# Second homes in dead attention buffers for the expert weights of one tile set, in an attention and mixture-of-experts kernel

## The chip, the cores and the metric

The kernel runs on one core of one Trainium2 chip. The metric is the device time of one execution in microseconds (us). Five engines run their own instruction streams and meet at semaphores: TensorE (PE; its weight loads are listed as PEld), VectorE (DVE), ScalarE (ACT), GpSimd (POOL) and SyncE (SP, which here only issues transfers). A name with q behind it (SPq, ACTq) is the engine's sequencer, where its transfers are issued. Sixteen DMA engines move the data of all queues.

## What is computed

The reference, cut to what matters (8 batches of 256 tokens with 256 features, 16 heads, 77 context keys, 16 experts with one expert per token):

```python
x = x + attention(layernorm(x), ctx, ctx, mask, Wq, bq, Wk, bk, Wv, bv, Wo, bo)
h = layernorm(x).reshape(2048, 256)
logits = h @ w_router.T                       # 16 experts
top = top_k(logits, 1)
scores = sigmoid(logits) * one_hot(top)
gate, up = split(scores.T[:, :, None] * h @ gate_up_proj)    # per expert: 256 -> 2 x 512
expert = (up * silu(gate)) @ down_proj                        # per expert: 512 -> 256
shared = silu(h @ w_gate.T) * (h @ w_up.T) @ w_down.T
x = x + (shared + expert.sum(axis=0)).reshape(8, 256, 256)
```

Everything is float32. With the reference's inputs the 16 experts get 109, 249, 79, 164, 51, 177, 57, 78, 162, 185, 87, 183, 101, 171, 104 and 91 tokens.

## The kernel before, in words

**Stages.** The first 205 us are the attention over eight batches, with the shared feed-forward of the first five batches (the "early" ones, NE = 5) woven in. Then come the shared products of the last three batches (R = 3) on PE (L778 gate and up, L790 down), beside which DVE works out the routing: where each token goes in tiles of 32 rows (TS) that belong to one expert each. Last come 20 expert steps (NSTEP).

**An expert step.** A step takes four tiles (NG) at a time, one in each quarter of PE's columns. The steps alternate between two sets of weight buffers: even steps use set A (a = 0), odd ones set B (a = 1). Step i is use u = i // 2 of its set. A set holds for each of its four tile lanes one expert's gate-and-up weights (128 x 2048 numbers, 1 MB, `w_egu`) and down weights (128 x 1024, 0.5 MB, `w_ed`). Set A lies in the buffers `own`, set B in the `arena` that attention used before. Set A's guess of the experts it will need is loaded in the attention (L307, L309 with a = 0), set B's once attention is over.

**SP's order.** SP issues, in program order, (1) the usual experts of set B, once the last attention product is out (L306 to L309); (2) after the routing is known, for use 0 of both sets the weights of those lanes whose expert differs from the guess (L337 gate and up, L342 down; each transfer carries a condition `new`, and where it is false nothing is moved, but the semaphore is raised); (3) for step i from 2 on: `gate_up_again(i)` waits until the gate-and-up products of step i - 2 have read the same buffers (`egu_psum`), `down_again(i)` until its down products have (`ed_psum`). Step i's gate and up are issued before step i - 1's down. Tiles lie in order of experts and a lane takes ten tiles in a row, so a lane's expert changes seldom. Worked out from the token counts above, the lanes with a new expert are, at uses 0 to 9: set A 2, 2, 1, 1, 2, 1, 0, 0, 0, 1; set B 1, 0, 0, 0, 0, 2, 1, 0, 0, 3.

**PE's order in the expert part.** For each step: gate and up (L862, 32 products), the previous step's down (L880, 32 products), the transposes of the next step's gathered rows (L851), and the transposes of its own hidden values (L869), for which ACT's gate and DVE's product of the same step must be done. The first products are gate-and-up 0, then L851 for step 1, L869 for step 0, gate-and-up 1, down 0, L851 for step 2, L869 for step 1, gate-and-up 2, down 1, L851 for step 3, L869 for step 2, gate-and-up 3, and so on.

**POOL's order in the expert part.** POOL issues three kinds of indirect transfers, each behind a small marker instruction (L493): `gather_rows` (L504) brings the normalised rows of a step into `xs`, `gather_base` (L512) the sums to which the result is added (`attT` is where they land), `scatter_out` (L519) writes the result. The order is rows 0, 1, 2, a wait for all eight stores of `base`, base 0, base 1, rows 3, scatter 0, base 2, rows 4, scatter 1, and so on.

**The base.** `base` is a DRAM copy of the sum of residual, attention and shared output. SP stores it for the five early batches (L301), ACT for the last three (L1021, 256 KB each, 128 x 2 pieces of 1 KB), each when DVE has added the shared output (`shared_added`). All eight raise `base_stored`.

**ACT's and DVE's orders.** ACT in the expert part: scale the rows of a step (L1031, waits for the gathered rows), gate of the step before (L1039), read out the transposed rows (L1035), read out the transposed hidden values (L1043). DVE: hidden values of step i (L1356), then the result rows of step i - 1 (L1363), which wait for the gathered base.

## Time and profile before

| what | value |
|---|---|
| time, median of 3 runs | 392.1 us (390.1 to 392.56) |
| profiled execution, its own time | 395.31 us |
| its span, first to last instruction | 393.3 us |
| mean granted TensorE clock | 0.980 of full |
| expert part on PE (first L862 to last L880) | 248.0 to 384.2 us |

A timeline row gives the start, the duration, engine, line, operation, what is written from what, how many instructions are merged, and in brackets how long the engine had been idle before and what ended that idle time. A row with "DMA own<-w_experts" in its brackets is one where PE stood and the transfer of expert weights came last. A windows row gives for a stretch of time the busy time of each engine, the granted TensorE clock as a share of full (1.00 is 2.4 GHz, 0.50 is 1.2 GHz), the busy share of the DMA engines and the bytes they moved per second.

### The profile page before, as it was taken

How to read it: one execution, taken by the hardware profiler on the slowest of the kernel's cores; microseconds unless marked ns; L12 is line 12 of the kernel's file. 1: busy time of each engine (PE TensorE's matmuls, PEld its weight loads, DVE VectorE, ACT ScalarE, POOL GpSimd, SP SyncE). 2: the span in 40 equal slices, each digit the busy share in tenths (PEclk: the TensorE clock that was granted, in tenths of full speed). 3: DMA queues.
4: the chain of work that ended last, by engine and by line, in shares of the span. 5: the costliest groups of instructions: out<-in, count | busy, mean ns of one | idle time of the engine just before them, and what ended most of it. 6: DMA issues, size and time to landing. Idle time of an engine off the chain costs nothing.

```text
span 393.3 us, 9350 instructions
## 1 busy us (share of the span) xinstructions
PE 352.2 (90%) x3068; PEld 225.3 (57%) x3068; DVE 191.6 (49%) x567; ACT 172.9 (44%) x472; POOL 159.5 (41%) x271
## 2 busy tenths in 40 slices
PE   2778788999999999998999999979998999999780
PEld 1556466777777777776776888424443434444330
DVE  2479899967967949767742852112121212111110
ACT  1258979665665565756641311312333232332310
POOL 5354656433522623422221021333656464656411
PEclk9989999999999999999999999989999999999987
DMA  8330102020069300000014999384558696314940
GB/s 239 145 85 3 44 0 72 0 72 2 27 231 408 125 0 27 27 26 3 27 55 168 397 273 363 114 343 147 184 163 287 223 350 209 106 41 159 380 197 20
DMA packets 23326, 56.47 MB, mean 144 GB/s; under 512 B 7275, under 2 KB 14461, under 8 KB 19968
## 3 DMA queue, kind: packets, MB, share of 16 engines
q1 hardware_dynamic: 16704, 48.59, 34.6%
q0 software_dynamic: 2880, 6.31, 5.0%
q10 hardware_dynamic: 3712, 1.22, 1.3%
q8 instruction: 13, 0.21, 0.2%
q14 instruction: 17, 0.14, 0.1%
HBM read 149.94 MB, written 6.82 MB: 399 GB/s over the span
## 4 chain that ended last, share of the span: by engine, by line
PE 30%; issue 27%; POOL 16%; DVE 13%; ACT 5%; DMA 5%; POOLq 1%; DVEq 0%; ACTq 0%
PE ps L651 8%; POOL xs L504 5%; POOL attT L512 5%; PE ps L657 5%; PE ps L578 4%; PE ps L593 3%; DMA rows<-score 3%; POOL pool_carrier L493 3%; POOL out L519 2%; PE ps L632 2%; DVE arena L1127 2%; PE ps L603 2%; ACT arena L935 2%; DVE den L1136 2%; DMA mask_in<-mask 2%
## 5 line engine op out<-in xcount | busy, mean ns | idle before, releaser
L451 POOL TENSOR_TENSOR arena<-arena,rden 128x308 f32<-128x308 f32 x64 | 44.7, 699 | 95.0 <-DVE rden L1140 94.3
L935 ACT ACTIVATE arena<-arena,negtop 128x77 f32<-128x77 f32 x256 | 70.6, 350 | 19.2 <-DVE negtop L1132 19.2
L1356 DVE TENSOR_TENSOR act_g<-act_g,ps 128x512 f32<-128x512 f32 x20 | 13.8, 688 | 90.9 <-PE ps L862 90.9
L493 POOL TENSOR_TENSOR pool_carrier<-neghalf 1x1 f32<-1x1 f32 x60 | 11.0, 183 | 81.2 <-DVE qT L1363 48.3
L603 PE MATMUL ps<-ident,arena 128*77 128x128 f32 x256 | 40.4, 284 | 2.1 <-ACT arena L943 2.1
L862 PE MATMUL ps<-own,qT 128*32 128x512 f32 x320 | 37.9, 615 | 4.4 <-DMA own<-w_experts 3.5
L862 PE MATMUL ps<-arena,qT 128*32 128x512 f32 x320 | 38.1, 617 | 3.8 <-DMA arena<-w_experts 3.6
L651 PE MATMUL ps<-xn2T,w_gu 128*128 (+1 forms) x160 | 39.5, 390 | 0.6 <-ACT xn2T L948 0.6
L603 PEld LDWEIGHTS ps<-ident,arena 128*77 128x77 f32 x256 | 30.0, 150 | 10.6 <-issue 6.7
L651 PEld LDWEIGHTS ps<-xn2T,w_gu 128*128 128x128 f32 x160 | 28.8, 189 | 10.0 <-issue 5.9
L1035 ACT ACTIVATE qT<-ps 128x256 f32<-128x256 f32 x20 | 7.7, 383 | 59.5 <-PE ps L851 59.5
L1127 DVE TENSOR_TENSOR arena<-ps,arena 128x308 f32<-128x308 f32 x64 | 30.0, 469 | 5.9 <-PE ps L593 5.6
L1136 DVE TENSOR_REDUCE den<-arena 128x4 f32<-128x308 f32 x64 | 29.7, 465 | 4.8 <-ACT arena L935 4.7
L593 PE MATMUL ps<-arena,qT 64*128 64x308 f32 x128 | 25.2, 471 | 6.3 <-DVE arena L1127 4.7
L1132 DVE TENSOR_REDUCE negtop<-arena 128x4 f32<-128x308 f32 x64 | 30.3, 474 | 0.1
L862 PEld LDWEIGHTS ps<-own,qT 128*32 128x32 f32 x320 | 10.9, 112 | 24.7 <-issue 20.8
L519 POOL DMA_INDIRECT out<-qT,token x20 | 20.4, 1020 | 11.3 <-issue 10.7
L862 PEld LDWEIGHTS ps<-arena,qT 128*32 128x32 f32 x320 | 9.6, 113 | 25.5 <-issue 19.5
L1039 ACT ACTIVATE act_g<-ps 128x512 f32<-128x512 f32 x20 | 11.9, 596 | 24.6 <-PE ps L862 24.5
L943 ACT ACTIVATE arena<-ps 77x512 f32<-77x512 f32 x32 | 18.7, 584 | 9.2 <-PE ps L603 9.2
L504 POOL DMA_INDIRECT xs<-rows,token x20 | 20.7, 1035 | 3.9 <-issue 1.7
L778 PE MATMUL ps<-xn2T,w_gu 128*128 128x256 f32 x96 | 22.2, 382 | 0.0
(149 smaller groups left out, 579.2 us busy)
## 6 DMA issues: line engine op xcount, KB each, us to landing
own<-w_experts SPq DMA_DIRECT2D x44, 1024.0 KB
arena<-w_experts SPq DMA_DIRECT2D x44, 1024.0 KB
own<-w_experts SPq DMA_DIRECT2D x44, 512.0 KB
arena<-w_experts SPq DMA_DIRECT2D x44, 512.0 KB
arena<-x SPq DMA_DIRECT2D x8, 256.0 KB, 3.1
rows<-xn_now SPq DMA_DIRECT2D x7, 256.0 KB, 2.7
base<-x SPq DMA_DIRECT2D x5, 256.0 KB, 2.1
arena<-w_qkvoT SPq DMA_DIRECT2D x4, 256.0 KB, 5.2
```

The source lines that it names most:

```text
L451: pool.tensor_tensor(prob[k][:, :, :], prob[k][:, :, :], rden[k][:, :].rearrange("p (h o) -> p h o", o=1).to_broadcast([P, HU, K]), ALU.mu ...
L493: pool.tensor_tensor(pool_carrier[:, i:i + 1], neghalf[0:1, 0:1], neghalf[0:1, 0:1], ALU.add).then_inc(parted[i], 1)
L504: pool.indirect_dma_start(xs[i % 2][:, :], None, rows, token_of(i), bounds_check=T - 1, oob_is_err=False).then_inc(xs_in[i % 2], 16)
L519: pool.indirect_dma_start(tokens, token_of(i), ys[i % 2], None, bounds_check=T - 1, oob_is_err=False).then_inc(ys_out[i % 2], 16)
L593: pe.matmul(ps[:, bank_s[g], 0:HU * K], qT[s][half, c, t * P:(t + 1) * P], kblk[s][half, c, :, :].rearrange("p h k -> p (h k)"), start=Tru ...
L603: mm = pe.transpose(ps[0:K, bank_pt[k % 2], h * P:(h + 1) * P], prob[k][:, h, :], ident[:, :])
L651: mm = pe.matmul(ps[:, bank, part * S:(part + 1) * S], w_gu[:, k, col:col + P], xn2T[:, k, bass.ds(g * S, S)], start=(k == 0), stop=(k == ...
L862: mm = pe.matmul(ps[c * TS:(c + 1) * TS, bank, 0:FF], xsT[:, k, c * TS:(c + 1) * TS], w_egu[a * NG + c][:, col:col + FF], start=(k == 0), ...
L935: ins = act.activation(prob[k][:, h, :], prob[k][:, h, :], ACT.Exp, bias=negtop[k][:, h:h + 1])
L1127: dve.tensor_tensor(prob[k][:, :, :], ps[:, bank_s[k % 2], 0:HU * K].rearrange("p (h k) -> p h k", h=HU), cap[s][:, t:t + 1, :].to_broadca ...
L1132: dve.tensor_reduce(negtop[k][:, :], prob[k][:, :, :], AX_X, ALU.max, negate=True).then_inc(s_top, 1)
L1136: dve.tensor_reduce(den[k][:, :], prob[k][:, :, :], AX_X, ALU.add).then_inc(den_ready, 1)
```

## The change

For every use of set A after its first (step 2, 4, 6, ...), the weights have other buffers than for step 0. Gate and up of the four lanes go to the two halves of `xn2T` (the transposed normalised rows, read last by the shared gate-and-up products), to `w_gu` (the shared gate-and-up weights) and to a new buffer `more_gu`. The down weights go to two pieces of `x1` that hold the first early batches (stored in `base` long before), to `w_d` (the shared down weights) and to a new `more_d`.

Since step 2's buffers are not those of step 0, its loads no longer wait for step 0's products. SP issues them right behind the corrections of use 0: `more_gu` at once, the other three gate-and-up loads when the last shared gate-and-up product is out (`gu_psum` at 12), then the down loads (after `base_stored` of the early batches), the last of them when the last shared down product is out (`d_psum` at 3). They carry no condition: all four lanes are loaded, also the two whose expert step 0 had already. From step 3 on the order is as before; steps 4, 6, ... load into the new buffers when step i - 2 has read them, with the condition.

`base_stored` is now raised by the five early stores only, and ACT's three stores raise a semaphore of their own, `base_last`; POOL waits for both where it waited for one.

```diff
+        more_gu, more_d = sb("more_gu", [P, gu_w]), sb("more_d", [P, d_w])
+        later_gu = [xn2T[:, 0, :], xn2T[:, 1, :], w_gu[:, :, :].rearrange("p c n -> p (c n)"), more_gu[:, :]]
+        later_d = [x1[:, 0:NTT // 4, :].rearrange("p t d -> p (t d)"), x1[:, NTT // 4:NTT // 2, :].rearrange("p t d -> p (t d)"),
+                   w_d[:, :, :].rearrange("p k d -> p (k d)"), more_d[:, :]]
...
-                    sp.dma_start(w_egu[a * NG + c], weights_of(at)[:, 0:gu_w], cond=new).then_inc(gu_in[a], 16)
+                homes, landed = (later_gu, later_gu_in) if a == 0 and u > 0 else (w_egu[a * NG:(a + 1) * NG], gu_in[a])
+                    sp.dma_start(homes[c], weights_of(at)[:, 0:gu_w], cond=new).then_inc(landed, 16)
...
-            now = gate_up_again(SETS)
-            for i in range(SETS, NSTEP - 1):
+            second = [at for at, new in wanted(0, 1)]
+            for c in (NG - 1, *range(NG - 1)):
+                if c == 0:
+                    sp.wait_ge(gu_psum, 4 * R)
+                sp.dma_start(later_gu[c], weights_of(second[c])[:, 0:gu_w]).then_inc(later_gu_in, 16)
+            sp.wait_ge(base_stored, 16 * NE)
+            for c in (NG - 1, *range(NG - 1)):
+                if c == 2:
+                    sp.wait_ge(d_psum, R)
+                sp.dma_start(later_d[c], weights_of(second[c])[:, gu_w:gu_w + d_w]).then_inc(later_d_in, 16)
+            now = gate_up_again(SETS + 1)
+            for i in range(SETS + 1, NSTEP - 1):
...
-            pool.wait_ge(base_stored, 16 * B)
+            pool.wait_ge(base_stored, 16 * NE)
+            pool.wait_ge(base_last, 16 * R)
...
-                pe.wait_ge(gu_in[a], 16 * NG * (u + 2))
+                if a == 0 and not (isinstance(u, int) and u == 0):
+                    homes = later_gu
+                    pe.wait_ge(later_gu_in, 16 * NG * u)
+                else:
+                    homes = w_egu[a * NG:(a + 1) * NG]
+                    pe.wait_ge(gu_in[a], 16 * NG * (u + 2))
...
-                              x1[:, QT * g:QT * (g + 1), :]).then_inc(base_stored, 16)
+                              x1[:, QT * g:QT * (g + 1), :]).then_inc(base_last, 16)
```

On SP, right behind the down corrections of use 0, the program before goes to step 2's conditional gate-and-up loads into `own`, the first of which stands here behind the wait for step 0's products (`TENSOR_LOAD step_word` reads which experts are wanted, `REGISTER_ALU` and `ISA` rows work out an address):

```order
L342 DMA arena<-w_experts 128x1024
L325 TENSOR_LOAD step_word
L325 ISA x2
L337 REGISTER_ALU [waits egu_psum]
L337 ISA
L337 REGISTER_ALU
L337 ISA
L337 DMA own<-w_experts 128x2048
```

At the same place in the changed program the loads for step 2 wait for nothing (`more_gu`), for the shared products (`gu_psum`) and for the early stores:

```order
L372 DMA more_gu<-w_experts 128x2048
L372 REGISTER_ALU [waits gu_psum]
L372 ISA
L372 DMA xn2T<-w_experts 128x2048
L372 REGISTER_ALU x2
L372 ISA
L372 DMA xn2T<-w_experts 128x2048
L372 REGISTER_ALU x2
L372 ISA
L372 DMA w_gu<-w_experts 128x2048
L377 ISA [waits base_stored]
L377 DMA more_d<-w_experts 128x1024
```

Behind these rows stand three more down loads, the last with a wait for `d_psum`, and then step 3's loads as before. What moved is that eight whole loads (6.3 MB) now stand ahead of the wait for the expert steps.

On POOL the order of the transfers stays; the marker ahead of base 0 now waits for two semaphores, and rows 3 still stand behind base 0 and base 1 (changed program):

```order
L521 DMA xs<-rows,token 128x257
L510 TENSOR_TENSOR pool_carrier<-neghalf 1x1 [waits base_last,base_stored]
L529 DMA attT<-base,token 128x256
L510 TENSOR_TENSOR pool_carrier<-neghalf 1x1 [waits parted1]
L529 DMA attT<-base,token 128x256
L510 TENSOR_TENSOR pool_carrier<-neghalf 1x1 [waits parted0,xsT_psum]
L521 DMA xs<-rows,token 128x257
```

Nothing moved here; lines are 17 further down than in the program before.

## Rows read from the trace of the kernel before

**Rows 1.** Page, busy time, share of the span and instructions of each engine.
```profile
PE 352.2 (90%) x3068; PEld 225.3 (57%) x3068; DVE 191.6 (49%) x567; ACT 172.9 (44%) x472; POOL 159.5 (41%) x271
```

**Rows 2.** Waits, 190 to 393 us: who waited for whom, us in total, times, longest.
```profile
PE ps L862 <- DMA arena<-w_experts: 3.6, 2, 2.7
PE ps L862 <- DMA own<-w_experts: 3.5, 2, 2.3
```

**Rows 3.** Timeline of PE, end of the shared products and first expert steps.
```profile
239.90 3.62 PE L778 MATMUL ps<-xn2T,w_gu 128*128 128x256 f32 x16
...
244.37 3.72 PE L790 MATMUL ps<-w_d,hT 128*128 128x256 f32 x16 [0.63 <-DVE hT L1280]
...
258.70 0.60 PE L869 MATMUL ps<-ident,act_g 128*128 128x128 f32 x4
261.60 5.15 PE L862 MATMUL ps<-own,qT 128*32 128x512 f32 x32 [2.30 <-DMA own<-w_experts]
266.57 1.90 PE L880 MATMUL ps<-arena,hT 128*32 128x256 f32 x32
268.40 0.44 PE L851 MATMUL ps<-ident,xs 128*128 128x128 f32 x2
...
269.31 3.64 PE L862 MATMUL ps<-arena,qT 128*32 128x512 f32 x32
...
275.61 3.64 PE L862 MATMUL ps<-own,qT 128*32 128x512 f32 x32
```

**Rows 4.** Timeline of PE, two later steps that waited for weights.
```profile
301.69 3.64 PE L862 MATMUL ps<-own,qT 128*32 128x512 f32 x32 [1.19 <-DMA own<-w_experts]
...
373.95 5.29 PE L862 MATMUL ps<-arena,qT 128*32 128x512 f32 x32 [2.66 <-DMA arena<-w_experts]
```

**Rows 5.** Timeline of SP's sequencer: issues of expert weights.
```profile
235.44 1.41 SPq L342 DMA_DIRECT2D arena<-w_experts  x4
252.12 2.36 SPq L337 DMA_DIRECT2D own<-w_experts  x4
257.22 2.27 SPq L337 DMA_DIRECT2D arena<-w_experts  x4
```

**Rows 6.** Windows: stretch, length, engines' busy us, granted clock, DMA share, GB/s.
```profile
236.00:242.00 6.00, 6.00 (x29) 5.29 (x28) 1.29 (x2) 0.17 (x1) 0.00 (x0) 1.00 1.01 413
...
244.00:248.00 4.00, 3.63 (x16) 2.96 (x16) 0.91 (x2) 0.15 (x1) 1.03 (x2) 1.00 0.54 177
...
253.00:261.00 8.00, 6.30 (x72) 2.62 (x70) 1.11 (x2) 2.57 (x5) 3.50 (x6) 1.00 0.82 309
261.00:266.00 5.00, 4.41 (x28) 1.16 (x32) 0.00 (x0) 1.11 (x2) 2.35 (x4) 0.66 0.80 279
```

**Rows 7.** Timeline of ACT's sequencer: two kinds of 256 KB stores.
```profile
215.25 0.41 ACTq L1003 DMA_DIRECT2D rows<-xn_now  x1
...
243.78 5.44 ACTq L1021 DMA_DIRECT2D base<-x  x3
```

**Rows 8.** Page, DMA issues: count, KB each, median us from issue to landing.
```profile
base<-x ACTq DMA_DIRECT2D x3, 256.0 KB, 2.2
...
xs<-rows,token POOLq DMA_INDIRECT x20, 3.5
...
rows<-xn_now ACTq DMA_DIRECT2D x1, 256.0 KB, 9.9
```

**Rows 9.** Timeline of POOL: base 0 and rows 3.
```profile
251.07 0.18 POOL L493 TENSOR_TENSOR pool_carrier<-neghalf 1x1 f32<-1x1 f32 x1 [5.53 <-DMA base<-x]
...
254.53 1.02 POOL L504 DMA_INDIRECT xs<-rows,token  x1
```

**Rows 10.** Timelines of ACT: scaled rows 3, gate 2.
```profile
261.05 0.51 ACT L1031 ACTIVATE xs<-xs 128x256 f32<-128x256 f32 x1 [1.12 <-DMA xs<-rows,token]
265.10 0.60 ACT L1039 ACTIVATE act_g<-ps 128x512 f32<-128x512 f32 x1 [3.54 <-PE ps L862]
```

**Rows 11.** Timeline of DVE: hidden values of step 2.
```profile
266.89 0.69 DVE L1356 TENSOR_TENSOR act_g<-act_g,ps 128x512 f32<-128x512 f32 x1 [7.91 <-PE ps L862]
```

More of the change, by code:

```diff
@@ L233, in xattn_moe @@
         score_ready = sem("score_ready")
+        later_gu_in, later_d_in = sem("later_gu_in"), sem("later_d_in")
         gu_in = [sem(f"gu_in{a}") for a in range(SETS)]
@@ L241, in xattn_moe @@
         xb_in = [sem(f"xb_in{s}") for s in range(2)]
[L242 removed]
+        base_stored, base_last, xb_init = sem("base_stored"), sem("base_last"), sem("xb_init")
         parted = [sem(f"parted{i}") for i in range(3)]
@@ L332, in weights_of, with load_gate_up, load_down @@
                 return flat[bass.ds(at, P * (gu_w + d_w))].rearrange("(p n) -> p n", p=P)
-            def load_gate_up(a, experts):
+            def load_gate_up(a, experts, u):
+                homes, landed = (later_gu, later_gu_in) if a == 0 and u > 0 else (w_egu[a * NG:(a + 1) * NG], gu_in[a])
                 for c, (at, new) in enumerate(experts):
-                    sp.dma_start(w_egu[a * NG + c], weights_of(at)[:, 0:gu_w], cond=new).then_inc(gu_in[a], 16)
-            def load_down(a, experts):
+                    sp.dma_start(homes[c], weights_of(at)[:, 0:gu_w], cond=new).then_inc(landed, 16)
+            def load_down(a, experts, u):
+                homes, landed = (later_d, later_d_in) if a == 0 and u > 0 else (w_ed[a * NG:(a + 1) * NG], d_in[a])
                 for c, (at, new) in enumerate(experts):
-                    sp.dma_start(w_ed[a * NG + c], weights_of(at)[:, gu_w:gu_w + d_w], cond=new).then_inc(d_in[a], 16)
+                    sp.dma_start(homes[c], weights_of(at)[:, gu_w:gu_w + d_w], cond=new).then_inc(landed, 16)
             first = [wanted(a, 0) for a in range(SETS)]
@@ L346, in _ @@
                 sp.wait_ge(gu_in[a], 16 * NG)
-                load_gate_up(a, first[a])
+                load_gate_up(a, first[a], 0)
             for a in range(SETS):
                 sp.wait_ge(d_in[a], 16 * NG)
-                load_down(a, first[a])
+                load_down(a, first[a], 0)
             def gate_up_again(i):
@@ L353, in gate_up_again @@
                 sp.wait_ge(egu_psum, i - SETS + 1)
-                load_gate_up(i % SETS, experts)
+                load_gate_up(i % SETS, experts, i // SETS)
                 return experts
@@ L862, in expert_gate_up @@
                             mm = pe.matmul(ps[c * TS:(c + 1) * TS, bank, 0:FF], xsT[:, k, c * TS:(c + 1) * TS],
-                                           w_egu[a * NG + c][:, col:col + FF], start=(k == 0), stop=(k == DC - 1))
+                                           homes[c][:, col:col + FF], start=(k == 0), stop=(k == DC - 1))
                     mm.then_inc(done, 1)
@@ L872, in expert_down @@
             def expert_down(i, a, u, first2):
-                pe.wait_ge(d_in[a], 16 * NG * (u + 2))
+                if a == 0 and not (isinstance(u, int) and u == 0):
+                    homes = later_d
+                    pe.wait_ge(later_d_in, 16 * NG * u)
+                else:
+                    homes = w_ed[a * NG:(a + 1) * NG]
+                    pe.wait_ge(d_in[a], 16 * NG * (u + 2))
                 pe.wait_ge(ehT_out, i + 1)
@@ L880, in expert_down @@
                         mm = pe.matmul(ps[c * TS:(c + 1) * TS, bank_d[a], 0:D], hT_e[:, k, c * TS:(c + 1) * TS],
-                                       w_ed[a * NG + c][:, k * D:(k + 1) * D], start=(k == 0), stop=(k == FC - 1))
+                                       homes[c][:, k * D:(k + 1) * D], start=(k == 0), stop=(k == FC - 1))
                 mm.then_inc(ed_psum, 1)
```

3 lines of the change are left out of this document (1 added, 2 removed).

## The prediction

> **What bounds the kernel now.** I read the page's busy times first: PE is busy for 90% of the span [rows 1], so only time in which PE stands can be won. The waits of the part behind the attention say where it stood for weights: four times, 7.1 us in all [rows 2]. PE's timeline puts them at steps 2, 8, 11 and 19; the three that matter are 2.30 us before step 2's gate and up, 1.19 us before step 8's and 2.66 us before step 19's [rows 3, 4]. Between them the expert part is a chain of PE work without a gap worth naming: from step 3's gate and up (269.31) to step 4's (275.61) is 6.30 us [rows 3]. Then I read the SP queue, the DMA share by window, and the timelines of ACT and POOL around step 2, to see what the new loads will meet there.
>
> **What the change can win.** SP issued step 2's loads when step 0's gate and up had been read, at 252.12 [rows 5]. Two of four lanes were new, 2.1 MB; the DMA engines moved 8 x 309 GB/s = 2.5 MB from 253 to 261 [rows 6], and PE could start at 261.60. It had been ready from 258.70 + 0.60 = 259.3 [rows 3]. The same 32 products then took 5.15 us where they take 3.64 [rows 3]: the granted clock was 0.66 of full from 261 to 266 [rows 6], so partly at 1.2 GHz, behind 2.3 us in which PE did nothing. If step 2's weights are there, both go: 2.30 + 1.51 = 3.8 us, and step 3's gate and up starts at 265.5 in place of 269.31. Nothing else is won: steps 8, 11 and 19 load behind the same waits as before, with the same conditions; steps 11 and 19 belong to set B, which the change leaves alone. The shorter issue list on SP is worth nothing, as SP waits there anyway.
>
> **Will step 2's weights be there?** SP is free at 235.44 + 1.41 = 236.9 [rows 5] and reads the next word; `more_gu` is issued at about 237.5. The three other gate-and-up loads follow when the last shared gate and up is out, 239.90 + 3.62 = 243.5 [rows 3], the down loads right behind, the last one at 244.37 + 3.72 = 248.1 [rows 3]. The DMA engines are full then (413 GB/s, share 1.01) and have worked off the corrections of use 0 at about 244 (share 0.54 from 244 to 248) [rows 6]. At 413 GB/s a gate-and-up load takes 2.6 us and a down load 1.3 us. So the weights' queue runs to 244 + 2.6 = 246.6 with `more_gu`, 254.4 with the other three, 259.5 with the down loads, and about 261.5 with the three base stores (0.79 MB, 1.9 us) in between. Gate and up land at about 256, 3 us before they are needed (259.3), and down at 261.5, needed after step 3's gate and up. Step 3's own loads are empty (no lane is new), and their semaphores come at the end of that queue, before 265.5. The stall in front of step 2 goes. The cover of these waits is 3 to 4 us.
>
> **What the new loads stand in the way of.** Before, the DMA engines were half idle from 244 to 248 [rows 6], and it is there that ACT's three base stores go: the first issued at 243.78, the last at 243.78 + 5.44 - 0.37 = 248.85 [rows 7], landing 2.2 us after issue [rows 8]. POOL waited for the last of them, until 251.07 [rows 9]. Now 6.3 MB of weights run beside them until 261. What a store of this size costs then is shown once: `rows<-xn_now`, 256 KB from the same queue, issued at 215.25 [rows 7] into the stream of set B's weights, took 9.9 us [rows 8] and not 2.2: 7.7 us more, the time of three 1 MB loads. The bounds for the landing L of the last store: not before 248.85 + 9.9 = 258.8 by that row alone; if all three stores, which stand behind each other in one queue, pay 7.7 us each beside the 1 MB loads and half of it beside the 0.5 MB loads, they are overtaken by the end of the stream and L is 262. I take **L = 260**, between the two, for the last 5 us of the stream are of the smaller loads. That is 9 us later than before.
>
> What is late next: base 0 and base 1 and behind them rows 3. Rows 3 were issued 254.53 - 251.07 = 3.46 us after the last store landed [rows 9], so now at 263.5. Before, they landed 6.5 us after issue, in the stream of step 2's weights (ACT's wait ended at 261.05 [rows 10]); the median of all is 3.5 us [rows 8]. By then the stream is over, but step 4's one new lane is issued at about 263.4, when gate-and-up 2 is out (259.3 + 3.6 = 262.9) (bounds 3.5 and 6.5; I take 4.5): 268.0. Then in a chain, ACT's scaling 0.51, its gate of step 2 behind it 0.60 [rows 10], DVE's product 0.69 [rows 11], L869's transposes 0.60 [rows 3], and 0.1 for hand-overs: **step 3's gate and up starts at 270.5**. PE will have been ready at 265.5, and waits 5 us. Before it was 269.31: 1.2 us later. The base sums themselves (base 0 lands at about 265) hold DVE's result of step 0, and through it hidden 2, less long than the gate does.
>
> The clock: PE stood 2.3 us before step 2 and lost 1.51 us, 2.66 us before step 19 and lost 5.29 - 3.64 = 1.65 [rows 3, 4]; the 1.19 us before step 8 cost nothing (3.64) [rows 4]. With 5 us step 3's gate and up will lose 1.6; before, it lost nothing.
>
> **Sum.** 1.2 + 1.6 = 2.8 us slower than the kernel before at the start of step 3's down, and the steps behind follow one for one: POOL needs 3.46 + 1.02 = 4.5 us for three transfers with their markers [rows 9] against PE's 6.3 per step and catches up. On the profiled execution's 395.31 us this is 398.1; that execution lies 3.2 us above the median of the runs shown, so on the median, 392.1, it is **394.9**.
>
> **One rule against this.** The row shows 9.9 us for a store in a stream of weights [rows 8]. The Trainium skill ("DMA: Bandwidth & Descriptors", section on queues, rings and completion order) says that each DMA engine takes turns between its queues and takes a whole packet, typically about 9 to 17 descriptors, at each turn. By it, a store (16 pieces of 1 KB per DMA engine) is one turn, and the first rival below follows. The measured 9.9 us fits two or three turns behind 1 MB loads better than one.
>
> **Rivals.** (1) *Stores slip through; faster.* Each store waits for one 1 MB load, 2.6 us, and goes: the first at about 249, the second at 252, the last at 255. Then rows 3 are issued at 258.5 and land by 263, step 3 starts at its 265.5, and all 3.8 us are won: 388.3. For it: a base store with free engines takes only 2.2 us. Against it: the 9.9 us. (2) *A draw.* The stores go a little earlier than I take: step 3 starts with L + 10.5; with L = 257.5 PE waits 2.5 us, pays the clock, and nothing is won, 392; at L = 256.5 it waits 1.5 us, pays no clock, and 2 us are won. (3) *Worse.* L = 262, rows 3 take 6.5 us beside step 4's load, step 3 starts at 274.5, 5.2 later than before, and with the clock's 1.6 that is 6.8: 398.9. (4) *It doesn't remove the stall*: the stores take so much of the stream that step 2's gate and up land after 259.3. It takes 3 us more than I find; then both stalls stand, 3 us on top of mine. The point from which slower decides is L of about 257.5.
>
> **How the numbers follow.** Mine (L from 258.5 to 262, 393 to 397) 0.50; rival 1 0.22; rival 2 0.13; rivals 3 and 4 together 0.15. The range takes in rival 1 and mine with its bounds: 388.2 to 397.8, leaving out most of 3 and 4. One per cent, 3.9 us, is about what a measurement of this kernel can tell from no change. Rival 1 wins 3.8, just below that, so faster by over 1% gets 0.09; slower by over 1% (396.0) takes the 0.15 and a quarter of mine's upper part, 0.25 in all; within 1% 0.66.
>
> **What the profile after would show.** Right: no idle before step 2's gate and up (then at 259.3, 3.64 us); DMA share near 1 from 244 to 260; `base<-x` from ACT at about 10 us to landing; POOL's marker of base 0 waiting until about 260; ACT's scaling of rows 3 ended by the gather at about 268; PE idle about 5 us before step 3's transposes, and then gate and up of over 5 us. Wrong: the stores landing in under 6 us, or the gap in front of step 3 missing.

## The result

The changed kernel takes 397.86 us in the median of four runs (396.11 to 398.23) against 392.33 us for the kernel before (390.1 to 392.67): a ratio of 1.0144, with a 95% interval of 1.0096 to 1.0193. It is 5.5 us slower, where 2.8 us were forecast (394.9 us); it lies 0.06 us above the upper end of the range. A second set of runs of the same kernel gave 1.0106 (1.0024 to 1.0188; e0 below). Ratios, here and below, leave out the few executions that ran over 1.5% longer than the fastest of their kernel.

| | before | changed |
|---|---|---|
| median | 392.33 us | 397.86 us |
| span of the profiled execution | 393.3 us | 396.4 us |
| start of the first expert products, called S below | 248.02 | 245.33 |
| last base store landed | S + 3.1 | S + 13.9 |
| step 2's gate and up starts | S + 13.6 | S + 11.4 |
| step 3's gate and up starts | S + 21.3 | S + 25.4 |
| step 3's gate and up lasts | 3.64 us | 6.05 us |
| step 2's down starts | S + 24.8 | S + 31.3 |
| last down starts | S + 134.3 | S + 140.0 |

The two profiled executions reach S 2.7 us apart. Ahead of that point the change only adds transfers, all the early loads but the last (`more_gu`'s is issued at S - 9.7); at S - 28, before any of them, both executions are already as far apart as at S. All comparisons are therefore made from S. From there on the changed kernel loses 5.7 us, which agrees with the 5.5 us between the medians.

The page of the changed kernel, the lines that answer to [rows 1, 8] (busy times, clock by 40 slices, and a part of the DMA queues: packets, MB, share of 16 engines):

```profile
PE 354.1 (89%) x3068; PEld 226.4 (57%) x3068; DVE 191.4 (48%) x567; ACT 172.7 (44%) x472; POOL 159.7 (40%) x271
...
PEclk9989999999999999999999999985999999999987
...
q1 hardware_dynamic: 17280, 51.74, 36.1%
```

PE is as busy as before. SP's queue (q1) moved 51.74 MB, 3.15 MB more than the 48.59 MB before: the two lanes that step 0 had already.

The waits after 190 us (who waited for whom, us in total, times, longest), which answer to [rows 2]:

```profile
POOL pool_carrier L510 <- DMA base<-x: 16.4, 1, 16.4
ACT xs L1059 <- DMA xs<-rows,token: 14.3, 4, 10.6
DVE qT L1391 <- DMA attT<-base,token: 7.9, 1, 7.9
PE ps L885 <- DMA arena<-w_experts: 3.1, 2, 2.5
...
PE ps L885 <- DMA more_gu<-w_experts: 0.9, 1, 0.9
```

The stall of PE on step 2's weights is gone; what is left on weights is steps 8, 11 and 19. In its place stand three waits on the chain from the base stores: POOL for the stores (5.5 us before), ACT for gathered rows, DVE for the gathered base.

The timeline of PE around steps 2 and 3, which answers to [rows 3] (step 2's products now read three buffers, so they print in many rows; the first is shown):

```profile
256.02 0.60 PE L892 MATMUL ps<-ident,act_g 128*128 128x128 f32 x4
256.75 0.62 PE L885 MATMUL ps<-xn2T,qT 128*32 128x512 f32 x2
...
260.18 1.94 PE L908 MATMUL ps<-arena,hT 128*32 128x256 f32 x32
268.46 0.69 PE L869 MATMUL ps<-ident,xs 128*128 128x128 f32 x2 [6.34 <-ACT xs L1059]
269.67 1.12 PE L892 MATMUL ps<-ident,act_g 128*128 128x128 f32 x4 [0.52 <-DVE act_g L1384]
270.71 6.05 PE L885 MATMUL ps<-arena,qT 128*32 128x512 f32 x32
```

Step 2 starts right behind the transposes, with no wait in brackets. Then PE stands for 6.34 us until ACT has scaled rows 3, and works on at a lower clock: the transposes take 1.12 us and not 0.60, step 3's gate and up 6.05 us and not 3.64.

POOL, ACT and DVE in the same stretch, which answer to [rows 9 to 11]:

```profile
259.25 0.18 POOL L510 TENSOR_TENSOR pool_carrier<-neghalf 1x1 f32<-1x1 f32 x1 [16.40 <-DMA base<-x]
...
262.72 1.02 POOL L521 DMA_INDIRECT xs<-rows,token  x1
```

```profile
267.90 0.51 ACT L1059 ACTIVATE xs<-xs 128x256 f32<-128x256 f32 x1 [10.65 <-DMA xs<-rows,token]
268.31 0.58 ACT L1067 ACTIVATE act_g<-ps 128x512 f32<-128x512 f32 x1
```

```profile
262.79 0.42 DVE L1391 TENSOR_TENSOR qT<-ps,attT 128x256 f32<-128x256 f32 x1 [7.88 <-DMA attT<-base,token]
268.92 0.69 DVE L1384 TENSOR_TENSOR act_g<-act_g,ps 128x512 f32<-128x512 f32 x1 [5.71 <-ACT act_g L1067]
```

This is the chain that was forecast: stores landed at 259.25, rows 3 issued 3.47 us later, there at 267.90, scaled, step 2's gate behind it, hidden 2, transposes, step 3. The landing of the three stores, from the rows on their line (us from issue to landing):

```profile
L1049 ACTq DMA_DIRECT2D base<-x x3: 366/366/428, 241.1 to 246.2; - x3
...
DMA to landing us min/median/max: 9.9/12.9/13.9
```

They took 2.2 us before [rows 8]. One by one, in the order of their issue, they took 9.9, 13.9 and 12.9 us and landed at S + 5.7, S + 10.8 and S + 13.7 (S + 13.9 in the table is where POOL goes on). And the windows, which answer to [rows 6]:

```profile
244.00:248.00 4.00, 4.00 (x35) 1.77 (x37) 0.69 (x1) 1.10 (x2) 0.00 (x0) 1.00 1.02 418
248.00:253.00 5.00, 4.49 (x42) 1.50 (x38) 0.69 (x1) 1.94 (x4) 0.00 (x0) 1.00 1.01 414
253.00:261.00 8.00, 7.87 (x98) 3.71 (x94) 0.69 (x1) 1.01 (x3) 1.20 (x2) 1.00 0.74 290
261.00:266.00 5.00, 1.11 (x23) 0.47 (x12) 0.42 (x1) 0.00 (x0) 4.30 (x8) 0.94 0.75 255
266.00:270.00 4.00, 1.02 (x4) 0.63 (x5) 1.02 (x2) 1.37 (x3) 1.75 (x3) 0.50 0.39 118
270.00:275.00 5.00, 5.00 (x27) 1.39 (x29) 0.00 (x0) 1.57 (x3) 3.62 (x6) 0.50 0.16 51
```

The DMA engines are full until about 258.5 = S + 13.2, and the last store lands with the end of that stream. The granted clock is 0.50, 1.2 GHz, from 266 to 275.

### The profile page after: what moved, and what is told of

It reads as the page before. It is cut to its first block, busy times and chain, and to the rows that moved or that the text cites. A ratio compares the mean times of both kernels' runs of the same rounds, so it can differ in the third digit from the quotient of the medians.

```text
span 396.4 us, 9351 instructions
## 1 busy us (share of the span) xinstructions
PE 354.1 (89%) x3068; PEld 226.4 (57%) x3068; DVE 191.4 (48%) x567; ACT 172.7 (44%) x472; POOL 159.7 (40%) x271
## 3 DMA queue, kind: packets, MB, share of 16 engines
q1 hardware_dynamic: 17280, 51.74, 36.1%
## 4 chain that ended last, share of the span: by engine, by line
PE 38%; issue 22%; POOL 15%; DVE 13%; ACT 5%; DMA 4%; POOLq 1%; DVEq 0%; ACTq 0%
PE ps L669 8%; PE ps L796 5%; POOL attT L529 5%; PE ps L675 5%; PE ps L596 4%; POOL xs L521 4%; DMA base<-x 3%; PE ps L611 3%; PE ps L808 3%; POOL pool_carrier L510 3%; POOL out L536 3%; PE ps L650 2%; DVE arena L1155 2%; PE ps L621 2%; ACT arena L963 2%
## 5 line engine op out<-in xcount | busy, mean ns | idle before, releaser
L963 ACT ACTIVATE arena<-arena,negtop 128x77 f32<-128x77 f32 x256 | 70.6, 350 | 19.3 <-DVE negtop L1160 19.3
L885 PE MATMUL ps<-arena,qT 128*32 128x512 f32 x320 | 40.5, 652 | 3.3 <-DMA arena<-w_experts 3.1
L885 PE MATMUL ps<-xn2T,qT 128*32 128x512 f32 x144 | 32.6, 594 | 1.9 <-DMA more_gu<-w_experts 0.9
L885 PE MATMUL ps<-more_gu,qT 128*32 128x512 f32 x72 | 32.6, 595 | 0.0
L885 PE MATMUL ps<-w_gu,qT 128*32 128x512 f32 x72 | 32.6, 595 | 0.0
L885 PEld LDWEIGHTS ps<-arena,qT 128*32 128x32 f32 x320 | 10.1, 118 | 26.9 <-issue 21.7
L971 ACT ACTIVATE arena<-ps 77x512 f32<-77x512 f32 x32 | 18.7, 583 | 9.2 <-PE ps L621 9.2
L1391 DVE TENSOR_TENSOR qT<-ps,attT 128x256 f32<-128x256 f32 x20 | 8.5, 425 | 28.7 <-PE ps L908 20.8
L521 POOL DMA_INDIRECT xs<-rows,token x20 | 20.7, 1034 | 3.9 <-issue 1.3
```

The lines of the kernel that those rows point to most:

```text
L521: pool.indirect_dma_start(xs[i % 2][:, :], None, rows, token_of(i), bounds_check=T - 1, oob_is_err=False).then_inc(xs_in[i % 2], 16)
L885: mm = pe.matmul(ps[c * TS:(c + 1) * TS, bank, 0:FF], xsT[:, k, c * TS:(c + 1) * TS], homes[c][:, col:col + FF], start=(k == 0), stop=(k = ...
L963: ins = act.activation(prob[k][:, h, :], prob[k][:, h, :], ACT.Exp, bias=negtop[k][:, h:h + 1])
```

## The experiments

Two theories were held against each other. Theory: the stream of eight early loads makes the last base stores late, these make rows 3 and base 0 late, and these PE. Rivals: the stream holds PE up itself, by the semaphores of step 3's empty loads; or the stores are late by something else than the stream. Times are read from each kernel's own S. Ratios are against the kernel before on the same chip: it took 394.4 us for e0, e5, e6 and e8, 400.7 for e1 to e4, 399.5 for e9 to e12, and 401.6 for e13 to e16. The changed kernel itself ran beside the first group only, so where another group is set against it, chips differ too, and the order of events from S says more than the ratio.

Where it took about 400 us (399.5 to 401.6), all traces but that of e2 show single waits of about 2 to 8 us in the expert part that are put down to no engine and no transfer of the kernel ("remote"); the traces of the two kernels above, and of e0, e5, e6 and e8, show none. They are taken up at the end.

### The changed kernel again (e0)

No edit.

> The changed kernel, unedited, on the chip of this call, so that the others have a neighbour. Both theories: about 1.4% over the kernel before; last store landed at S + 14 to S + 15, step 3's gate and up at about S + 25.

Ratio 1.0106 (1.0024 to 1.0188). The last store landed at S + 13.9, PE waited 5.82 us, step 3's gate and up started at S + 24.9. Up to step 3's start the order of events repeats to half a microsecond. Its gate and up took 5.25 us here and not 6.05, so step 2's down came at S + 29.9, where the first trace has S + 31.3.

### Rows 3 ahead of the stores (e1, e14)

```diff
+            gather_rows(3)
             pool.wait_ge(base_stored, 16 * NE)
             pool.wait_ge(base_last, 16 * R)
             gather_base(0)
...
-                if 3 <= i + 2 < NSTEP:
+                if 4 <= i + 2 < NSTEP:
```

> The changed kernel with one edit on POOL: rows 3 are gathered ahead of the wait for the base stores. Times are counted from S, the start of the first expert products (245.33 in the changed kernel's trace); there the last store lands at S + 13.9, rows 3 at S + 22.6, step 3's gate and up starts at S + 25.4 (before: S + 21.3; without any wait: S + 17.6). Theory (late stores hold up rows 3, and these PE): the stores land as late as before, S + 13.9, but rows 3 are there by S + 13; what is left is base 0 -> DVE's result of step 0 -> hidden 2, so step 3 starts at about S + 19.3 and PE's clock stays up: about 389 us, 8 to 9 under the changed kernel and 3 under the kernel before. Rival (the stream of weights itself, by the semaphores of step 3's empty loads, holds PE): the start of step 3 stays within 1 us of S + 25.4, about 397.9 us.

Measured: 1.0001 (0.9962 to 1.0040). As fast as the kernel before, and so better than the changed one, but without the 8 to 9 us that were expected. Step 3 started at S + 23.8: DVE's wait for base 0 ended only at S + 21.6, 6.0 us after its issue, and DVE wrote hidden 2 behind it. Since other waits of this trace have no known cause, it was run again.

> The changed kernel with rows 3 ahead of the base wait alone, once more, since its first trace had waits that no engine, semaphore or transfer of the kernel explains. Theory: base 0 lands at S + 17.4 as in the changed kernel, DVE writes hidden 2 behind it, step 3 starts at S + 19.3, step 4 at about S + 26.5 (rows 4): about as the kernel before. Rival: step 3 starts at S + 23 or later again.

Measured: 0.9967 (0.9925 to 1.0010). The timeline of DVE, then of PE:

```profile
264.31 0.43 DVE L1392 TENSOR_TENSOR qT<-ps,attT 128x256 f32<-128x256 f32 x1 [8.60 <-DMA attT<-base,token]
264.65 0.68 DVE L1385 TENSOR_TENSOR act_g<-act_g,ps 128x512 f32<-128x512 f32 x1
```

```profile
263.04 0.44 PE L870 MATMUL ps<-ident,xs 128*128 128x128 f32 x2
265.38 0.65 PE L893 MATMUL ps<-ident,act_g 128*128 128x128 f32 x4 [1.90 <-DVE act_g L1385]
```

S is 246.13 here. Rows 3 no longer hold anything (L870 follows without a wait). What is left is the second way: base 0 lands at S + 18.2, DVE's result of step 0 has waited 8.60 us for it, hidden 2 stands behind it, PE waits 1.90 us. Step 3 starts at S + 19.8 (19.3 expected) and the stores land as late as ever, S + 14.6. Step 4 started at S + 29.1 behind rows 4 and waits without a known cause, later than the S + 26.5 expected. Step 2 itself waited 0.33 us for the load into `w_gu`, until S + 11.6.

### Both ways cut, the stores left late (e13)

As above, and on DVE:

```diff
                 expert_hidden(2 * m + 1)
-                expert_rows(2 * m, 0, m, first)
-                expert_hidden(2 * m + 2)
+                if first:
+                    expert_hidden(2 * m + 2)
+                    expert_rows(2 * m, 0, m, first)
+                else:
+                    expert_rows(2 * m, 0, m, first)
+                    expert_hidden(2 * m + 2)
                 expert_rows(2 * m + 1, 1, m, first)
```

> The changed kernel with rows 3 ahead of the base wait, and on DVE the hidden values of step 2 ahead of the result of step 0. The stream of weights and the base stores stay as they are. Theory (the late stores reach PE by two ways only, rows 3 and base 0 through DVE's order): the last store still lands at about S + 14, but step 3's gate and up starts at S + 17.6 as if nothing were late. The result of step 0 is then done at S + 17.5 and rows 4, which POOL issues behind scatter 0 and base 2, land at about S + 26, so step 4 starts about 2.5 us late, at S + 26.5, against S + 27.6 in the kernel before: 0.2% to 0.4% under before. Rival (a third way, for example the semaphores of the empty loads behind the stream): step 3 starts at S + 19 or later.

```profile
260.98 1.94 PE L909 MATMUL ps<-arena,hT 128*32 128x256 f32 x32
262.84 0.44 PE L870 MATMUL ps<-ident,xs 128*128 128x128 f32 x2
263.12 0.60 PE L893 MATMUL ps<-ident,act_g 128*128 128x128 f32 x4
265.05 3.64 PE L886 MATMUL ps<-arena,qT 128*32 128x512 f32 x32 [1.33 <-ACT qT L1064]
```

S is 246.13 and the last store landed at S + 14.8. The transposes of rows 3 and of hidden 2 follow each other with no wait in front: neither way holds PE any more. Step 3 started at S + 18.9 and not 17.6, because ACT read out the transposed rows 1.3 us late, at 264.61; no semaphore explains that (the transposes had ended at 263.3). S + 18.9 is only just short of the rival's S + 19; what speaks against a third way is that PE's only wait in front of step 3 is for ACT, with the stream as long as ever. The four executions spread from 395.2 to 404.5 us, too far to read a time from, and the trace is of a long one (404.05 us), so only its order of events is used.

### The down loads held back behind the stores (e2), and with rows 3 ahead (e3)

```diff
             sp.wait_ge(base_stored, 16 * NE)
+            sp.wait_ge(base_last, 16 * R)
             for c in (NG - 1, *range(NG - 1)):
```

> The changed kernel with one edit on SP: the four early down loads wait until the last three base stores have landed. Theory (the stores are late because 6.3 MB of weights share the DMA engines with them): with 2.1 MB of the stream held back the stores land when the gate-and-up loads are through, S + 7 to S + 9 in place of S + 13.9; rows 3 are issued at S + 12, land beside the down loads at S + 17, step 3 starts at S + 19.5 to S + 20 and PE loses no or little clock: 389 to 390 us. Rival (what delays a store is its own queue or its three predecessors, not the stream): the last store lands at S + 12 or later and the time stays above 396.

Measured: 1.0027 (0.9998 to 1.0056). The last store landed at S + 10.5, 3.4 us earlier than in the changed kernel, but not at S + 7 to 9. Each still took 9.6 to 11.7 us; the gate-and-up loads kept the DMA engines full until about S + 8.5. Then the 2.1 MB that had been held back ran into the gathers: base 0 took 6.1 us to land and rows 3 6.5, step 3 started at S + 23.3, its gate and up took 5.15 us. Of the 3.4 us that the stores gained, step 3 kept 1.6 (against e0) to 2.1 (against the first trace); the rest was given back one link further.

> Both edits: rows 3 ahead of the base wait, and the early down loads behind the base stores. Theory: no wait in front of step 3 at all, its gate and up starts at S + 17.6, and the whole 3.7 us are won that the stall in front of step 2 cost the kernel before: 388.6 us. If something else than rows 3 and base 0 stands between, for example the down weights of step 2 coming late now, step 3's down or gate and up shows a wait on weights: 390 to 392.

Measured: 0.9975 (0.9941 to 1.0009). The timeline of DVE:

```profile
263.68 0.42 DVE L1393 TENSOR_TENSOR qT<-ps,attT 128x256 f32<-128x256 f32 x1 [9.51 <-DMA attT<-base,token]
```

Base 0 was issued at 255.79 and landed 7.9 us later, behind the held-back loads; step 3 started at S + 20.7 (S is 244.59), step 4 was late behind rows 4 and a wait of ACT with no known cause, at S + 30.0. The theory "no wait at all" failed: a gather of 128 KB pays in the stream as a store does.

### Half the stream (e4)

```diff
-            second = [at for at, new in wanted(0, 1)]
+            second = wanted(0, 1)
...
-                sp.dma_start(later_gu[c], weights_of(second[c])[:, 0:gu_w]).then_inc(later_gu_in, 16)
+                sp.dma_start(later_gu[c], weights_of(second[c][0])[:, 0:gu_w], cond=second[c][1]).then_inc(later_gu_in, 16)
```

(and the same for the down loads)

> The changed kernel with the condition kept on the eight early loads, so that only the two lanes with a new expert are moved (3.1 MB in place of 6.3). The other two lanes compute step 2 and later ones with whatever their new buffers hold, so the output isn't the reference's; the work and the waits are the same. Theory (the length of the stream sets when the stores land): the stream is 7.7 us shorter, the last store lands at S + 6 to S + 7, rows 3 at S + 14, step 3 starts at S + 17.6: 388.6 us. Rival (the loads' being early at all hurts, whatever their size, by their order against the stores): the last store still lands at S + 11 or later, above 394.

Measured: 0.9898 (0.9864 to 0.9931), where 388.6 against 392.3 us, 0.9905, had been expected: 1.0% faster than before, with the loads just as early and only half as long. The last store landed at S + 8.3 (6 to 7 expected). The trace itself is marred by a wait of ACT with no known cause in front of step 2, and step 3 started at S + 21.9 and not S + 17.6; it is read for the stores alone. The rival, that being early hurts whatever the size, falls.

### How the stores stand to the stream and to each other (e8, e11, e10)

In e8 SP issues the first two of the three stores in its own queue, ACT only the third:

```diff
+            store_last(NE)
             second = [at for at, new in wanted(0, 1)]
...
+            store_last(NE + 1)
             sp.wait_ge(base_stored, 16 * NE)
...
-            for g in range(NE, B):
-                store_base(g)
+            store_base(B - 1)
```

(`store_last(g)` is ACT's `store_base(g)` on SP)

> The changed kernel with the first two of the last three base stores issued by SP in the weights' queue; ACT issues only the third, at S + 0.9 as ever. Rows 3 stay behind the base wait. It measures whether the stores' standing behind each other in ACT's queue makes the last one late. Theory (each store in a queue of its own pays 7.7 us): it lands 9.9 us after its issue, at S + 10.8, 3 to 4 us earlier than in the changed kernel, and step 3 starts 3 to 4 us earlier: 0.3% to 0.7% over before. Rival (every store lands only when the stream of weights ends): S + 14, 1.4% over before.

```profile
246.69 0.37 ACTq L1056 DMA_DIRECT2D base<-x  x1
```

```profile
256.73 0.18 POOL L517 TENSOR_TENSOR pool_carrier<-neghalf 1x1 f32<-1x1 f32 x1 [13.35 <-DMA base<-x]
```

The lone store took 9.9 us from issue and POOL was released at S + 10.9 (S is 245.85), as the theory said to a tenth. In the changed kernel the same store, issued at S + 0.8 too, was there at S + 13.9. So of its 10.8 us of delay against the kernel before 7.7 are its own way through the stream and 3 are its two predecessors in ACT's queue. It did not wait for the stream to end, as the rival had it: the DMA engines stayed full for 3 us more, until about S + 14. Ratio 0.9978 (0.9935 to 1.0021), step 3 at S + 19.7: 5.2 us earlier than in e0, more than expected. 3.0 are the store; 1.7 are rows 3, which took 2.9 us to land and not 4.6; the rest is the transposes in front of step 3, which ran at full clock. Base 0 gained nothing more: issued while the stream still ran, it took 4.5 us and not 2.8.

In e11 and e10 each early gate-and-up load is cut in two transfers of 512 KB; e11's are made of 4 KB pieces, e10's of 2 KB pieces, where the changed kernel's are 8 KB.

```diff
+                into = later_gu[c].rearrange("p (a b n) -> p b a n", a=2, b=2)
+                source = weights_of(second[c])[:, 0:gu_w].rearrange("p (a b n) -> p b a n", a=2, b=2)
+                for b in range(2):
+                    sp.dma_start(into[:, b], source[:, b]).then_inc(later_gu_in, 16)
```

(e10; in e11 the halves are contiguous, `"p (b n) -> p b n"`; in both, PE's wait counts the four transfers more)

> The changed kernel with each of the four early gate-and-up loads cut into two transfers of 512 KB, each of 128 x 2 pieces of 2 KB (every other 2 KB block). The same bytes. It asks by what a DMA engine takes turns between ACT's store and SP's stream. If it takes turns piece by piece (so many pieces of the stream for one piece of the store, whatever their size), the first base store, 16 pieces of 1 KB per DMA engine, pays a quarter of its 7.7 us beside 8 KB pieces, and lands at about 4 us after issue. If it takes turns by transfers or large blocks, it pays as much as with pieces of 4 KB at the same transfer size.

> The same cut into two transfers of 512 KB, each of 128 pieces of 4 KB (first and second half). If turns go piece by piece, the first base store pays half of 7.7 us and lands at about 6 us after issue, later than with pieces of 2 KB; if by transfers, it also lands at about 6 us, but then with pieces of 2 KB too. If only bytes count, all three land at 9.9 us. In both kernels the last store lands earlier than S + 13.9 if the first does, at the latest with the end of the stream.

Us from issue to landing of the three stores, e11 and then e10:

```profile
DMA to landing us min/median/max: 7.8/9.3/10.0
```

```profile
DMA to landing us min/median/max: 6.4/7.0/7.8
```

| pieces of the gate-and-up loads | stores, issue to landing (min/median/max) | last store landed |
|---|---|---|
| 8 KB, 1 MB transfers (changed) | 9.9/12.9/13.9 | S + 13.9 |
| 4 KB, 512 KB transfers (e11) | 7.8/9.3/10.0 | S + 10.2 |
| 2 KB, 512 KB transfers (e10) | 6.4/7.0/7.8 | S + 7.4 |

The first of the three stores, of which the expectations speak, took 9.9, 7.8 and 7.0 us; about 6 and 4 had been expected if turns go piece by piece. The last took 12.9, 9.3 and 6.4 us. So with the same bytes, and at the same transfer size, smaller pieces let the stores through earlier, and neither bytes alone nor transfers alone set the turns. In proportion to the piece it is not either, and for the first store the step from 4 to 2 KB is small, 0.8 us; by what rule turns are taken stays open. Each is one execution (e10 397.3 us, e11 395.4, against a median of 399.5 for the kernel before), which is no verdict on the time. In e10 step 2 started 1.7 us late; whether the smaller pieces gave the stores so much of the DMA engines that weights came late, the trace does not tell, for it puts the wait down to ACT.

### The stores in the weights' own queue (e5, e12, e16)

Rows 3 ahead as in e1, and all three stores on SP: the first ahead of `more_gu`, the other two between the gate-and-up and the down loads.

```diff
+            store_last(NE)
             second = [at for at, new in wanted(0, 1)]
...
+            store_last(NE + 1)
+            store_last(NE + 2)
             sp.wait_ge(base_stored, 16 * NE)
...
-            for g in range(NE, B):
-                store_base(g)
             act.wait_ge(h_ready, 2 * R)
```

> The changed kernel with rows 3 gathered ahead of the base wait, and the last three base stores issued by SP in the same queue as the weights: the first ahead of more_gu, the other two behind the gate-and-up loads and ahead of the down loads. ACT issues none. Theory (a store in ACT's queue pays two or three 1 MB loads of the stream for itself, one in SP's queue only what stands ahead of it): the last store lands when the gate-and-up loads are through, S + 7 to S + 9, the down loads follow at once; base 0 is in by S + 15, step 3 starts at S + 17.6 to S + 19, and the whole stall of the kernel before is won: 0.9% to 1.0% under before. Rival (base 0's own gather pays for the down loads as a store does, as it did with both edits, 7.9 us): base 0 is in at S + 16 or later, step 3 starts at S + 19 to S + 21, 0 to 0.5% under before.

Measured: 0.9903 (0.9867 to 0.9940), 390.2 us. The timeline of PE:

```profile
262.15 1.94 PE L917 MATMUL ps<-arena,hT 128*32 128x256 f32 x32
264.02 0.44 PE L878 MATMUL ps<-ident,xs 128*128 128x128 f32 x2
264.78 0.66 PE L901 MATMUL ps<-ident,act_g 128*128 128x128 f32 x4 [0.32 <-DVE act_g L1391]
265.37 3.64 PE L894 MATMUL ps<-arena,qT 128*32 128x512 f32 x32
```

S is 247.32: step 3 started at S + 18.1, 3.2 us earlier than in the kernel before, at full clock. The last store landed at S + 10.8, later than the S + 7 to 9 expected, but 3 us earlier than in the changed kernel, and DVE had base 0 at S + 16.4, so that PE waited 0.32 us. How long the three stores took on their line:

```profile
L370 SPq DMA_DIRECT2D base<-x x3: 382/391/425, 237.3 to 248.1; - x3
...
DMA to landing us min/median/max: 8.7/9.9/11.3
```

In the order of issue it was 8.7, 11.3 and 9.9 us. The last one, issued at S + 0.8, took in the weights' queue just what e8's lone store took in ACT's, 9.9 us, and landed at the same point. So the queue as such won nothing for it; what both kernels have is no other store in ACT's queue ahead of it. What e5 has over e8, step 3 at S + 18.1 and not 19.7, is therefore put down to rows 3 ahead; no run has e8 with that edit alone.

The 1.0% is not all the stall in front of step 2. In this trace step 4 starts 2.0 us earlier than in the kernel before, counted from S (rows 4 are late, 25.6 against 27.6), the waits at steps 8 and 11 are together 1.0 us shorter, and step 19's products ran at full clock behind 2.66 us without work, where the kernel before lost 1.65 us; no edit aims at either. Twice more:

> The kernel with the stores on SP once more, as a neighbour for the one with the rows earlier. 0.9% to 1.0% under before, last store at about S + 10.8, step 3 at S + 18.

> Stores on SP and rows 3 ahead, as the neighbour of the others. Step 3 at S + 18, step 4 at S + 25.6, 0.9% to 1.0% under before.

0.9958 (0.9921 to 0.9995) and 0.9879 (0.9812 to 0.9946), with step 3 at S + 17.6 and S + 18.2 and the last store at S + 10.5 and S + 11.3; step 4 started at S + 26.9 and S + 27.5, later than the S + 25.6 expected. This version is 0.4% to 1.2% faster than the kernel before in three comparisons, each interval clear of 1. On the one chip where the changed kernel ran too, that one was 1.1% slower than the kernel before (e0) and this one 1.0% faster.

### The order of rows 3 in the kernel before (e6)

> The kernel before with rows 3 gathered ahead of the base wait, nothing else. If the order of rows 3 costs something only where the stores are late, as in the changed kernel, this one is the same as before within 0.3%: step 2 still starts at S + 13.6 behind its weights, step 3 at S + 21.3. If the order is a gain of its own, it is 1 us or more faster.

Measured: 1.0045 (1.0004 to 1.0086), no gain and perhaps a small loss. Step 2 still waited for its weights, here 2.90 us, and step 3 started at S + 22.1. So the POOL order is worth nothing where the stores are early.

### Every step's rows one position earlier (e9, e15)

```diff
-                if 3 <= i + 2 < NSTEP:
-                    gather_rows(i + 2)
+                if 4 <= i + 3 < NSTEP:
+                    gather_rows(i + 3)
```

(on top of e5)

> The kernel with the stores on SP, with POOL gathering every step's rows one position earlier still (rows 4 ahead of scatter 0, rows 5 ahead of scatter 1, and so on). There, with only rows 3 ahead, step 4's gate and up starts 1.2 us late since rows 4 are issued behind scatter 0 and base 2, at S + 20.5. Theory: rows 4 are issued at about S + 14.5, step 4 starts at S + 24.3 in place of S + 25.6; 1 to 1.3 us (0.3%) under the kernel with the stores on SP, about 1.2% to 1.3% under before. Rival (POOL's queue is then late with base 2 or the scatters, and DVE's results wait): no gain, or 1 us lost.

> Stores on SP and every step's rows one position earlier, once more, for the same reason. Theory: step 3 at S + 18, step 4 at S + 24.3, 1 us or more under the kernel with the stores on SP alone. Rival: no gain over it.

Measured: 1.0008 (0.9973 to 1.0043), beside e12's 0.9958, and 0.9949 (0.9905 to 0.9993), beside e16's 0.9879. Both times 0.5% to 0.7% slower than their neighbour, with intervals that overlap; both times with step 3 on time (S + 17.6 and S + 17.8) and step 4 late (S + 27.5 and S + 28.4, the neighbours S + 26.9 and S + 27.5), behind waits that no part of the kernel explains; e15:

```profile
ACT qT L1072 <- remote: 7.6, 1, 7.6
DVE qT L1398 <- remote: 5.8, 1, 5.8
```

Rows 4 did what was expected of them (step 4's first transposes had no wait, at S + 22.9 and S + 23.1), but the gain did not come. In both traces POOL stood 5.33 and 3.70 us in front of scatter 0 with no releaser named, where e12 and e16 have 0.61 us, and base 2 behind it was issued at S + 23.2 and S + 21.9 in place of S + 18.7 and S + 19.3. That is what the rival named, a late queue of POOL. Whether the order itself brings these waits about, or the chip, stays open: neither run was on a chip free of them.

## Why the prediction was off, point by point

**PE bound, the stall in front of step 2, what it is worth.** Right. Step 2 started without a wait, at S + 11.4 against S + 13.6, and its products ran at full clock. In e5 step 3 started 3.2 of the 3.8 us earlier, in e12 3.7. That e5's median ratio also comes to 3.8 us is partly luck, as said there.

**Weights there in time.** Right: gate and up, the down loads and step 3's empty loads were in before PE asked for them. The stream ended at S + 13.2; forecast from the 248.02 of the rows, 261.5 = S + 13.5. The cover of 3 to 4 us in front of step 2 is not shown: the traces do not give the landing of these loads, and in e14 PE waited 0.33 us for one of them.

**What the loads stand in the way of.** Right in kind, too small in size. The terms, from S:

| term | forecast | measured |
|---|---|---|
| last store lands | S + 12.0 (L = 260) | S + 13.9 |
| stores landed to rows 3 issued | 3.46 | 3.47 |
| rows 3, issue to landing | 4.5 | 5.2 |
| rows 3 landed to step 3's gate and up | 2.5 | 2.8 |
| step 3's start, later than before by | 1.2 | 4.1 |
| loss to the clock in it | 1.6 | 2.4 |
| step 2's down, later by | 2.8 | 6.5 |

The step that failed is the sentence that takes L = 260 "between the two". The upper bound of that step, three stores that pay one behind the other until the stream ends, gave 262 = S + 14.0, and that is what happened: the first landed 9.9 us after its issue, the second 5.2 us after the first, the third 2.9 us after the second, with the end of the stream. e8 shows why the lower bound was none: 9.9 us is the price of a store that is alone in its queue, and the changed kernel has three. The forecast's lower bound applied the price of one store to the last of a queue. That term is 1.9 us of the 3.7 that the sum missed. With it alone put right the sum would have been 394.9 + 1.9 = 396.8 us, inside the range; the terms below carried the time beyond it.

The second is the clock, 0.8 us. It was priced by idle times of 2.3 and 2.66 us [rows 3, 4]; with 6.34 us the transposes in front of step 3 ran at 1.2 GHz already (that is the 0.3 us in the row above it) and its gate and up lost 2.41. In e0, the same kernel with 5.82 us without work, they lost 1.61, just the forecast's 1.6. Across the runs the loss does not go by the length of the wait alone: behind 2.66 us it was nothing in e5, behind 2.67 us it was 2.97 in e8. The third is rows 3's landing, 0.7 us, inside its bounds.

Behind step 2's down 0.8 us of the 6.5 came back: the waits in front of steps 8, 11 and 19 were shorter (0.89, 0.59 and 2.48 us against 1.19, 0.93 and 2.66). Why is not shown; a late PE is not what it takes, for in e5, where PE is early, those at steps 8 and 11 are shorter as well (0.88 and 0.28). The forecast had steps 8 to 19 follow one for one.

**The range.** 397.8 was short by 0.06 us. The case that came lies between the forecast's own upper bound (L = 262, rows 3 in 4.5 us, 397) and rival 3, "worse" (L = 262, rows 3 in 6.5 us, 398.9); rows 3 took 5.2. The range had left most of rival 3 out. 0.15 for rivals 3 and 4 together was too small, as L = 262 was the upper bound that the forecast's own reasoning had worked out.

**The rule.** The rule on turns by packets was weighed against the 9.9 us of one store and given rival 1 with 0.22. The runs go against rival 1: the last store landed at S + 13.9 and not S + 7, and e8's lone store repeated the 9.9 us, 7.7 more than with free DMA engines, where rival 1 had 2.6. The Trainium skill ("DMA: Bandwidth & Descriptors", section on queues, rings and completion order) has the DMA engines take turns by packets of about 9 to 17 descriptors. e10 and e11 agree with it in that smaller pieces let a store through sooner at the same transfer size. An estimate from the Trainium skill's figure on that page: 17 pieces of 8 KB per engine are one turn of about 5.4 us at 413 GB/s over 16 engines, less than the 7.7 us measured, so a store of 16 pieces per engine seems to take more than one turn; no run here counts the turns.

**The two ways to PE.** The forecast named rows 3 first and base 0 through DVE as "less long". e14 and e13 show both, and the size: with the first cut, PE waits 1.90 us for the second; with both cut, for neither.

## What to carry to other kernels

A load that is issued early runs beside something else. Before moving one, list the small transfers in the same stretch, in whichever queue, that others wait for, and price each by a row of the trace in which such a transfer met such a stream; where several stand in one queue, their delays add, up to the end of the stream. Two things paid here: not leaving several waited-for stores behind each other in a second queue (e8, e5), and moving gathers that do not need the stores ahead of the wait for them (e14, e5). Which queue the last store went through made no difference: 9.9 us in either, in one trace each (e8, e5).

## What the runs showed of the hardware

- A store of 256 KB (256 pieces of 1 KB) took 9.9 us from another queue beside a stream of 8 KB pieces at 410 GB/s, with free DMA engines 2.1 to 2.7 us; three in a row 9.9, 13.9 and 12.9. From the stream's own queue the store issued at the same point took 9.9 us as well (e5). Beside pieces of 4 KB the last of three landed 3.7 us earlier, beside 2 KB 6.5 us earlier.
- Gathers of 128 KB pay likewise: base 0 landed 2.8 us after issue when the stream was over (changed kernel), 4.8 us beside the down loads (e5), 6.1 and 7.9 us directly behind 2.1 MB of them (e2, e3).
- The clock: after 2.3 us without work 32 products took 5.15 us, after 2.66 us 5.29, after 5.82 us 5.25 (e0), after 6.34 us 6.05; after 1.19 us 3.64. Step 19's products took 3.64 us behind the same 2.66 us without work in e5 and behind 3.31 us in e16, but 6.61 us behind 2.67 us in e8, so a wait of that length can cost nothing or 3 us.
- Single waits of about 2 to 8 us that the trace puts down to nothing of the kernel, in 11 of 12 traces from the two chips where the kernel before took about 400 us and in none of 6 others. Most stand in the first steps of the expert part; e10 and e11 have one of 5.6 us at about S + 93 too. What they are stays open.
